# Graph-network kernel: a row pair's statistics one step at a time, pair 0's products three steps later, and the left scores sent between two adjacency loads

## What is computed

```
deg = max(rowsum(adj), 1)
h = relu(layernorm(x))
# layer 0
sums = adj @ h;  gate_a = sigmoid([sums, h] @ Wa.T + ba);  gate_b = sigmoid([sums, h] @ Wb.T + bb)
g = h @ W_sa;  e = where(adj, exp(-leaky_relu(g @ a_left [:, None] + g @ a_right [None, :], 0.01)), 0)
x = x + sigmoid(gate_a * (e / (rowsum(e) + 1e-5)) @ g + gate_b * (adj @ (h @ W_gcnb) + b_gcnb))
# layer 1
h = relu(layernorm(x));  x = x + relu((D^-1/2 (adj + I) D^-1/2 h + h) @ W + b)
```

## Time and profile before

| | |
|---|---|
| median of 3 runs | 609.82 us (609.41 to 611.63) |
| the profiled execution: its own time, its span | 611.8 us, 610.0 us |
| PE busy | 593.4 us, 97% of the span |
| DVE, ACT, POOL busy | 425.2 us (70%), 362.4 us (59%), 255.5 us (42%) |

### The profile page before, as it was taken

How to read it: one execution, slowest core, us unless ns; L and a number is a source line. 1 busy time by engine, 2 the same in 40 slices (tenths; PEclk the granted TensorE clock), 3 DMA queues, 4 the chain that set the end, 5 groups by cost and what they waited for, 6 DMA issues and landing times.

```text
span 610.0 us, 13250 instructions
## 1 busy us (share of the span) xinstructions
PE 593.4 (97%) x5265; PEld 508.4 (83%) x5265; DVE 425.2 (70%) x811; ACT 362.4 (59%) x878; POOL 255.5 (42%) x361
## 2 busy tenths in 40 slices
PE   7889998999999999999999999999999999999996
PEld 5446687888888888888888888888888888888886
DVE  6897885999998999899989989988753121111111
ACT  3687667797887979797979788979642000000000
POOL 3664313554453435343525276313132374435433
PEclk8999999899999999999999999999999999999999
DMA  8908399957566565647474745010400486546401
GB/s 198 225 3 113 111 134 249 203 83 182 94 150 121 123 134 110 146 98 162 81 177 67 190 52 79 2 19 1 130 2 18 113 318 215 174 157 193 144 20 35
DMA packets 55801, 73.60 MB, mean 121 GB/s; under 512 B 20027, under 2 KB 47933, under 8 KB 54331
## 3 DMA queue, kind: packets, MB, share of 16 engines
q0 software_dynamic: 28544, 22.15, 26.5%
q1 hardware_dynamic: 24754, 46.42, 23.5%
q10 hardware_dynamic: 2441, 4.20, 2.2%
HBM read 69.31 MB, written 22.16 MB: 150 GB/s over the span
## 4 chain that ended last, share of the span: by engine, by line
PE 82%; DVE 5%; DMA 4%; issue 4%; POOL 4%; ACT 2%; ACTq 0%; POOLq 0%; DVEq 0%
PE accE L786 11%; PE accE L788 11%; PE accE L787 11%; PE accA L764 10%; PE accA L765 10%; PE accA L831 7%; PE accA L830 7%; PE accE L830 4%; PE accE L831 4%; DMA stage<-in_adj_dram 3%; POOL stage L369 1%; DVE bst L933 1%; PE pw L803 1%; PE accA L847 1%; PE pw L805 1%
## 5 line engine op out<-in xcount | busy, mean ns | idle before, releaser
L786 PE MATMUL accE<-HI,Z 128*128 128x257 f16 x676 | 185.2, 274 | 2.4 <-DVE wm L1078 2.1
L788 PE MATMUL accE<-HI,E 128*128 128x257 f16 x676 | 184.8, 273 | 0.0
L787 PE MATMUL accE<-LO,Z 128*128 128x256 f16 x676 | 184.7, 273 | 0.0
L549 ACT ACTIVATE Z<-LO,sr 128x256 f32<-128x256 f32 x338 | 151.4, 497 | 35.6 <-PE accE L788 35.6
L764 PE MATMUL accA<-HI,adjT 128*128 128x260 f16 x676 | 154.0, 273 | 0.0
L765 PE MATMUL accA<-LO,adjT 128*128 128x258 f16 x676 | 154.0, 273 | 0.0
L558 ACT ACTIVATE Z<-Z,sr 128x256 f32<-128x256 f32 x338 | 150.1, 496 | 0.2
L1034 DVE TENSOR_TENSOR Z<-adjT,Z 128x512 f32<-128x512 bf16 x169 | 127.0, 751 | 17.1 <-ACT Z L558 16.1
L1040 DVE TENSOR_TENSOR E<-Z 128x512 bf16<-128x512 f32 x169 | 129.0, 763 | 5.8
L369 POOL DMA_DIRECT2D stage<-in_adj_dram x96 | 59.3, 649 | 93.0 <-DVE adjT L1026 88.6
L831 PE MATMUL accA<-LO,adjT 128*128 128x256 f16 x416 | 91.6, 273 | 0.0
(11 more groups left out here) (127 smaller groups left out, 721.0 us busy)
## 6 DMA issues: line engine op xcount, KB each, us to landing
adjT_store<-adjT SPq DMA_DIRECT2D x11, 1664.0 KB, 6.3
stage<-in_adj_dram POOLq DMA_DIRECT2D x48, 192.0 KB, 5.0
stage<-in_adj_dram POOLq DMA_DIRECT2D x36, 224.0 KB, 5.2
adjT<-adjT_store SPq DMA_DIRECT2D x7, 896.0 KB, 6.0
adjT<-adjT_store SPq DMA_DIRECT2D x7, 768.0 KB, 6.0
stage<-adjT_store SPq DMA_DIRECT2D x4, 896.0 KB, 6.4
stage<-adjT_store SPq DMA_DIRECT2D x4, 768.0 KB, 5.8
out_dram<-late ACTq DMA_DIRECT2D x11, 256.0 KB
```

Source lines behind the costliest of these rows:

```text
L549: ins = act.activation(Z[:, n % RING, v], slw[:, m], ACT.Relu, bias=sr99[:, t:t + 1], scale=1.0 - SLOPE)
L786: pe.matmul(dst[:, 0:D + 1], zhi, HI[:, t, 0:D + 1], start=(t == 0), stop=False)
L787: pe.matmul(dst[:, 0:D], zhi, LO[:, t, 0:D], start=False, stop=False)
L788: ins = pe.matmul(dst[:, 0:D + 1], zlo, HI[:, t, 0:D + 1], start=False, stop=(t == TILES - 1))
```

## The change

It does five things. The statistics of one row pair a step replace two a step with the inverse deviations in batches. Everything of pair 0 in the second part (its turns of the adjacency, its blocks, `neighbours` and `unit`) comes three steps later (BEHIND = 9 in place of 6), with the adjacency loads and turns that follow it. The steps 0 to 2 are ordered anew: `turn(i + 1)` and `project(0)` stand between the two halves of `dense`. SP sends group 0 of the left scores between the loads of pair 0 and pair 1 and not after pair 1's. And m = 1's first blocks are begun on ACT and DVE before pair 0's gates, with nbias made early on POOL and DVE's `turn_adj(2, c)` placed among them.

```diff
-    BATCHES = [(0, 1), (1, 2), (2, 3), (3, 4), (4, 5), (5, 7), (7, 9), (9, PAIRS)]
+    BEHIND = 9
...
+            sp.wait_ge(adj_in[1], adj_count(0, 1))
+            spread_left(0)
             sp.wait_ge(adj_in[1], adj_count(1, 1))
-            spread_left(0)
             keep_adj(0)
             spread_left(1)
...
             load_adj(0, 1)
-            loads = {6: (1, 0), 7: (1, 1), 11: (2, 0), 12: (2, 1)}
+            pool.wait_ge(bias_in, 32)
+            pool.tensor_scalar(nbias[:], bias2[:], -1.0, None, ALU.mult).then_inc(nbias_ok, 1)
+            inv_std(3)
+            inv_std(4)
+            loads = {BEHIND: (1, 0), BEHIND + 1: (1, 1)}
             for s in range(PAIRS):
                 score_parts(s)
...
                 gate_columns(s)
+                if s >= 1 and s + 4 < PAIRS:
+                    inv_std(s + 4)
                 if s in loads:
                     load_adj(*loads[s])
+            load_adj(2, 0)
+            load_adj(2, 1)
...
-            act.wait_ge(srw_ok, PAIRS)
-            act.activation(el[:], srw[:, :, 3], ACT.Exp, scale=SLOPE).then_inc(el_ok, 1)
-            gate_exp(0)
-            gated_b(0)
...
+                    if m == 1 and u == 3:
+                        gate_exp(0)
+                    if m == 1 and u == 5:
+                        gated_b(0)
...
                 for e in range(2):
+                    if i <= 1 and e == 1:
+                        turn(i + 1)
+                    if i == 1 and e == 1:
+                        project(0)
...
-                if s >= 6:
-                    neighbours(0, s - 6)
-                if s >= 7:
-                    unit(0, s - 7)
+                if s >= BEHIND:
+                    neighbours(0, s - BEHIND)
+                if s > BEHIND:
+                    unit(0, s - BEHIND - 1)
...
-            turns = {5: (0, 0), 6: (0, 1), 10: (1, 0), 11: (1, 1)}
+            turns = {BEHIND - 1: (0, 0), BEHIND: (0, 1), PAIRS: (1, 0), PAIRS + 1: (1, 1)}
...
-                for j in (2 * s + 3, 2 * s + 4):
-                    if j < PAIRS:
-                        row_stats(j)
+                if s + 4 < PAIRS:
+                    row_stats(s + 4)
...
-            turn_adj(2, 0)
-            gate_args(0)
-            gates(0)
...
+                    if m == 1 and u == 1:
+                        gate_args(0)
+                    if m == 1 and u == 2:
+                        turn_adj(2, 0)
+                    if m == 1 and u == 3:
+                        gates(0)
+                    if u == (6 if m == 1 else 4):
                         row_sums(m - 1)
```

More of the change, by code:

```diff
@@ L515, in turned @@
                 act.wait_ge(hT_ps, i + 1)
+                if 2 <= i <= 3:
+                    act.wait_ge(proj, i - 1)
                 if i >= 2:
@@ L859, in _ @@
                 if s == 0:
-                    turn(1)
-                    project(0)
+                    keep_busy(5)
+                if s == 1:
                     spread_weights(2, 4, 2)
-                    keep_busy(4)
-                if s == 1:
+                    turn(3)
+                    project(1)
+                if s == 2:
+                    project(2)
                     widen_first()
-                if s + 2 < PAIRS:
+                if 2 <= s and s + 2 < PAIRS:
                     turn(s + 2)
@@ L938, in row_stats, with minus_mean @@
                 ins.then_inc(stats, 1)
[L940 to L943, removed]
+            def minus_mean(i):
+                dve.wait_ge(rstd_ok, i + 1)
+                dve.scalar_tensor_tensor(out=nmr[:, i], in0=mv[:, i, :, 0], scalar=-1.0, in1=rstd[:, i],
                                          op0=ALU.mult, op1=ALU.mult).then_inc(nmr_ok, 1)
@@ L1003, in diagonal_first, with second_half @@
                 ins.then_inc(diag_ok, 1)
[L1005 to L1011, removed]
+            def second_half(i, e):
+                dve.wait_ge(hi_ok, 2 * i + e + 1)
+                first = bass.AP(HI[:].tensor, (2 * i + e) * HIW, [[TILES * HIW, P], [G0, 2], [1, D]])
+                dve.tensor_tensor(LO[:, 2 * i + e, 0:2 * D].rearrange("p (k d) -> p k d", k=2),
+                                  bank(dn, e).rearrange("p (k d) -> p k d", k=2), first,
+                                  ALU.subtract).then_inc(lo_ok, 1)
             def turn_adj(m, c):
@@ L1129, in _ @@
             row_stats(2)
+            second_half(0, 0)
+            minus_mean(2)
+            turned_second(1)
+            second_half(0, 1)
             dve.wait_ge(w1_in, 16)
@@ L1132, in _ @@
             on_diagonal(2, 4)
-            second_halves(0)
-            minus_mean(2)
+            row_stats(3)
             take_scores(0)
[L1136 to L1139, removed]
             row_stats(4)
             minus_mean(3)
-            turns = {5: (0, 0), 6: (0, 1), 10: (1, 0), 11: (1, 1)}
-            for s in range(1, PAIRS + 6):
-                if s < PAIRS:
+            scales(2, 4, 2)
+            diagonal_first()
+            turns = {BEHIND - 1: (0, 0), BEHIND: (0, 1), PAIRS: (1, 0), PAIRS + 1: (1, 1)}
+            for s in range(1, PAIRS + BEHIND):
+                if 2 < s < PAIRS:
                     take_scores(s)
```

94 lines of the change are left out of this document (45 added, 49 removed).

## The result

The changed kernel took **615.21 us** (median of 7 runs, 612.82 to 616.78) against 610.8 us (7 runs of the kernel before beside it, 609.41 to 612.52): a ratio of **1.0064, 95% interval 1.0046 to 1.0082**. Forecast were 607.4 us and a range of 604.3 to 610.4. The profiled execution took 612.82 us with a span of 611.0; it is the shortest of the seven, so the trace shows less of the loss than the median. An execution whose mean granted clock was 1.000 took 615.21 us, the median, so a low clock is not what makes the loss.

What follows compares the result with a forecast made beforehand. PE, busy 97% of the span, bounds the kernel; only waits and low clock can be won. unit(1, 0) 1.1 us earlier plus 1.7 us of clock gave -2.8 us, span 607.2; median taken as 607.4, range 604.3 to 610.4.

Steps and rivals of the forecast that it cites:

- The step that failed: Behind 110 us PE was taken to be fed without a gap, so only the start and clock of unit(1, 0) counted.
- the price of the later start: Up to the end of pair 1's neighbours, the part was to grow by about 1.1 us, to 105.4 from 104.3.
- the 1.7 us of low clock: TensorE work lost at 104 to 113 us behind the wait for wm; it was to be won back.
- The first three steps: From 14.69 us: a new 2.5 us PE wait for hTx to 22.6, another 0.6 ahead of dense(1).
- the 0.9 us that were to be won there: dense(4) was to start at 32.0 us against 32.88 before, 0.9 us early.
- Steps 4 to 10 and the tail: No waits in steps 4 to 8, then 1.5 and 1.1 us at pair 0's turns, 0.6 and 1.1 in the tail.
- The wm chain: From gate_args(0) at T = 91.2, wm would let PE start at T + 12.6, so it is no longer waited for.
- 1.6 us in hand: Slack of the wm chain: PE is busy until 105.4, T + 14.2, while wm allows a start at T + 12.6.
- Rival 1: PE still waits for wm if its chain is over 1.6 us longer: 609 to 610.5 us, chance 0.16.
- rival 3: The low clock moves to the new wait at 20.1 to 22.6 us; 1.7 us come back: 609.1, chance 0.11.
- Rival 4: Slower: early second scores store lets re-read and pair 1's storing precede pair 2's load; landing at 98.6 gives 612.9; chance 0.07.
- rival 2: First part better than counted: 604.8 us if half its waits go, 603.5 without the first and the tail's; chance 0.20.

Runs made afterwards that it cites:

- p: l with gate_args(1), gate_exp(1) and gates(1) moved later as in the change: 611.0 us, ratio 1.000 to the kernel before.
- l: m with the rework of m = 1's start added, gates(1) left in place: 608.7 us, ratio 0.996 to the kernel before.
- e: The changed kernel with steps 0 to 2 back in the order of before: 613.45 us, ratio 1.004 to the kernel before.
- g: e with pair 1's gates also back at their places of before: 610.9 us, ratio 1.000 to the kernel before.
- a1: The changed kernel measured and profiled once more, unchanged: 615.5 us, ratio 1.009 to the kernel before.
- b: The changed kernel with only pair 1's gates back at their places of before: 612.7 us, ratio 1.003 to the kernel before.
- c: The kernel before with only nbias made early, right behind pair 0's adjacency load: 609.2 us, ratio 0.998 to the kernel before.
- h: c with one pair's statistics a step in place of two: 608.1 us, ratio 0.996 to the kernel before.
- k: h with pair 0's work in the second part three steps later (BEHIND = 9): 612.5 us, ratio 1.003 to the kernel before.
- o: k with group 0 of the left scores sent between the adjacency loads: 614.3 us, ratio 1.006 to the kernel before.
- f: The changed kernel with pair 1's storing held for pair 2's first chunk and the second scores store behind pair 2's storing: 619.45 us, ratio 1.013.
- m: h with group 0 of the left scores sent between the adjacency loads: 608.8 us, ratio 0.996 to the kernel before.
- n: h with pair 0's work one step later (BEHIND = 7): 610.3 us, ratio 1.000 to the kernel before.

## Why the prediction was wrong

**The step that failed**: "From there on PE is fed without a gap, and the change leaves the loops for m of 2 and more as they are." The sum stopped at `unit(1, 0)`, but the change goes on in m = 1: it moves gates(1), gate_args(1) and gate_exp(1). This costs 1.02 + 1.42 = 2.4 us in the trace after, and 2.4 to 2.8 us by p against l, e against g and a1 against b. No rival had it. From `unit(1, 0)` to the end of the span b, c, g and h take 501.8 us and the kernel after, a1 and e 504.2 to 504.3; the kernel before takes 503.5 with its 1.7 us of low clock. Two terms failed beside it: the price of the later start was put at 1.1 us and measured 4.3 (k over h), and the 1.7 us of low clock were taken as a gain of the median, though at least 51 of 92 executions of the kernel before have no such fall (c above).

**The difference of the spans.** Forecast was a span of 607.2 and it was 611.0, 3.8 us more. 2.4 are the two waits in m = 1. Another 0.9 us: pair 1's neighbours end at 106.3 and not at 105.4, 0.5 of it from the later first `dense`. The last 0.5 us is a wait for wm that was to be gone. The medians differ by more, 615.2 against 607.4: another 2.4 us lie between the changed kernel's profile and its median, and its first steps alone take 2.7 us more in a1's profile than in this one; and 1.6 us were taken off before's profiled execution to come to a median.

**The first three steps.** Forecast: a wait of 2.5 us and one of 0.6; it was 2.96 and 0.61. The 0.5 us is a step of DVE's queue that the forecast had as never waiting, the statistics of pair 4, which waited for their rows of x. DVE's timeline after:

```profile
20.61 0.75 DVE L947 BATCH_NORM_STATS2 bst<-xs 128x6 f32<-128x256 f32 x2 [0.70 <-DMA xs<-in_x_dram]
...
22.72 0.68 DVE L1003 TENSOR_TENSOR hTx<-tp,hTx 128x512 f16<-128x512 f32 x1
```

In a1 that wait is 1.51 us. `dense(2)`, `dense(3)` and `dense(4)` came at 24.66, 29.22 and 32.88 (forecast 23.7, 28.2, 32.0). Before, `dense(4)` came at 32.88, too, so the 0.9 us that were to be won there were not.

**Steps 4 to 10 and the tail.** None in 4 to 8, right. 1.5 and 1.1 us forecast, 1.85 and 1.13 measured; in the tail 0.6 and 1.1, measured 0.66 and 1.10. So "about 1.1 us longer" was right in sign. But the later start has a second price that the sum did not have: pair 2's first turn is late, by the storing of adjT in k and by its load in o, and with it the gates and wm, by 4 us and more.

**The wm chain.** "1.6 us in hand" was forecast, and a wait of 0.49 us remained. Two links were longer, by DVE's timeline after:

```profile
95.11 1.84 DVE L1038 STREAM_TRANSPOSE adjT<-stage 128x768 uint32<-128x768 uint32 x2 [1.08 <-DMA stage<-in_adj_dram]
...
102.11 1.75 DVE L1052 TENSOR_TENSOR E<-Z 128x512 bf16<-128x512 f32 x1
```

The chunk came 1.1 us after DVE wanted it, and one split took 1.75 us where it usually takes 0.69, beside POOL's `with_bias`. 1.08 + 1.06 = 2.1 us, where the forecast had put in 0.7. In a1 the wait for the chunk was 2.17 us and wm was 1.58 us late. So the profiled execution kept its full clock at 107, as forecast; g had a wait of 2 us there.

**Rivals.** Rival 1 (wm still waited for) is there at 0.5 to 1.6 us, rival 3 (low clock behind the new wait) in the profiles of a1, b and f. Rival 4's sign, a landing of pair 2's chunk behind 94, came true: 95.08 in the kernel after, 94.24 in o. What was behind it was not quite what the rival said: the second store, issued at 68.24, was not early through but ran beside the load until 81.9, and then the re-read and pair 1's storing ran beside it. It had a chance of 0.07. In the kernel after the rework of m = 1 hides most of it (1.08 us of waiting for the chunk, 2.17 in a1). In rival 2, the time without the first wait and the tail's is 607.4 - 2.5 - 1.7 = 603.2 by its own terms, not 603.5; nothing hangs on it.

**The whole by parts**, each as the difference of two ratios in the table times 610.6 us: nbias early -1.2, one statistic a step -1.5, pair 0 later +4.8, early scores +1.8, the rework of m = 1 -3.7, gates(1) moved +2.4, the new order of the first steps +2.8. Each is good to about 1.6 us; by construction they add up to a1's +5.4. The rework of m = 1 does a part of what was forecast of it: the wait for wm falls from 4.4 us (o) to 2.1 (g), and the low clock behind it is gone. But the whole of that wait came with the later start, since h has none; in the kernel before, two moved lines for nbias take the wait that was there, and on top of these the rework is worth nothing (l against m).

## What to carry to other kernels

Follow a change to its last edited line: the gates moved far behind the disputed wait cost as much as the whole forecast gain. Before a piece of work is begun later, follow its buffers: who stores them away, who loads them anew, what stands ahead of both in their queues, and who is held where they are used next. And try the smallest edit that removes the named waits first: two edits of a few lines, which take the last link (nbias) out of the chain and the second statistic out of a step, gave 608.1 us, and no kernel here is faster than that beyond the noise.

## What the runs showed of the hardware

**The length of a wait did not decide whether the clock fell.** From full it fell to half (PEclk 0.50, the 1.2 GHz level) behind waits of 2.2 us (before), 2.6 (b and f), 3.8 (a1), 4.2 (k), 4.4 (o) and 4.6 us (f, at 137), and stayed at full behind one of 2.96 us (the kernel after, profiled) and two of 2.1 us (g at 105, h at 47). The Trainium skill (TensorE: Matmul & The Clock Gate, What's actually happening) says that the periods run free of the kernel's start; that the same wait of the same kernel shows a fall in a1's profile and none in the first agrees with it, though the two waits were not equally long.

**A 6 KB store in 4-byte pieces took 10 to 26 us.** The row of the second store in before's transfers from 60 to 125 us:

```profile
sl_store<-srw SPq DMA_DIRECT2D x1, 6.0 KB, 19.2
```

It took 20.3 us in f, 13.1 in m and 26.3 in n, and the first store of before took 11.8. SP waits for it, so everything behind it in SP's queue starts later. Loads beside it took longer. f shows this at two places, against the kernel after: pair 2's first four pieces, with the store taken away and pair 1's storing held, have a median of 4.5 us in place of 12.8; pair 3's, issued at 113 to 115 us in both kernels and in f with the store beside them, land 11.0 to 17.5 us after their issue in place of 8.1 to 9.7.
